# Batch-norm sums of a GNN kernel: products of a tile with itself on TensorE in place of column sums of values and squares

## What is computed

```python
h = a * x + node_out              # (N, D)
mu = h.mean(0)
var = h.var(0)
x = x + (h - mu) / jnp.sqrt(var + EPS) * g + be
```

## Time and profile before

| | |
|---|---|
| time, median of 3 runs | 6509.96 us (6462.72 to 6547.05) |
| span of the profiled execution | 5432.4 us |
| busy in it: PE, DVE, ACT, POOL | 4063.8 (75%), 3799.0 (70%), 2766.8 (51%), 3340.6 (61%) |
| statistics of layer 0, first to last DVE pass | 839.0 to 1003.5 us |
| statistics of layer 1, first to last DVE pass | 1787.3 to 1952.5 us |
| mean granted TensorE clock | 0.877 of full speed |

### The profile page before, as it was taken

The page is one execution under the profiler, slowest core; times in us unless marked ns, Lnnn a source line. Parts: engine busy times, 40 slices in busy tenths (PEclk is TensorE's granted clock), DMA queues, the critical chain, the costliest instruction groups (busy, mean ns, idle before and its releaser), DMA issues. The chain is left out here.

```text
span 5432.4 us, 61024 instructions
## 1 busy us (share of the span) xinstructions
PE 4063.8 (75%) x14777; PEld 2245.4 (41%) x14777; DVE 3799.0 (70%) x7522; ACT 2766.8 (51%) x5374; POOL 3340.6 (61%) x3399
## 2 busy tenths in 40 slices
PE   7854548402444866556989999999999989995697
PEld 4522223101222334444556555655565544553343
DVE  8986663698666368885878767876787677762276
ACT  7952222212222246656978547844784477544433
POOL 6757777776777737774357735700670066777677
PEclk9977669756776988888999999999999999997899
DMA  6743237884111789885878546754775377874455
GB/s 215 270 161 100 94 110 255 294 283 152 47 46 46 260 270 266 260 239 188 271 231 257 189 140 222 251 181 134 231 253 175 134 246 238 277 223 137 140 179 163
DMA packets 628091, 1062.84 MB, mean 196 GB/s; under 512 B 105048, under 2 KB 258158, under 8 KB 627740
## 3 DMA queue, kind: packets, MB, share of 16 engines
q1 hardware_dynamic: 498972, 818.46, 46.2%
q0 software_dynamic: 100544, 163.41, 10.8%
q10 hardware_dynamic: 28224, 77.08, 3.6%
HBM read 599.34 MB, written 464.81 MB: 196 GB/s over the span
## 5 line engine op out<-in xcount | busy, mean ns | idle before, releaser
L1891 POOL DMA_INDIRECT G<-msg_tab,srow x784 | 739.9, 944 | 914.2 <-issue 813.2
L878 PE MATMUL l_ps<-cv_V,cv_cwi 128*128 128x448 f32 x896 | 475.4, 698 | 769.4 <-DVEq L865 769.4
L878 PEld LDWEIGHTS l_ps<-cv_V,cv_cwi 128*128 128x128 f32 x896 | 218.9, 252 | 1026.4 <-issue 538.5
L1285 POOL DMA_INDIRECT x_tab<-a_r,node_pos x392 | 379.6, 968 | 200.6 <-issue 115.9
L2152 DVE TENSOR_TENSOR agg<-r_psS,agg 128x128 f32 x980 | 280.9, 287 | 285.2 <-PE r_psS L1998 211.8
L747 POOL DMA_INDIRECT o_tab<-cv_ob,put_idx x392 | 387.8, 989 | 122.8 <-issue 118.5
L1972 PE MATMUL r_psR<-r_hin,whh 128*128 128x512 f32 x882 | 454.1, 597 | 0.9 <-ACT r_ohn L2071 0.9
L739 POOL DMA_INDIRECT cv_M<-h_tab,gat_src x392 | 373.8, 953 | 119.4 <-issue 119.4
L1923 PEld LDWEIGHTS r_psM<-wmsg,r_hnew 128*128 128x128 f32 x2744 | 361.1, 192 | 169.6 <-issue 140.4
L1998 PE MATMUL r_psS<-r_sel,G 128*128 128x128 f32 x1960 | 297.7, 300 | 132.0 <-DMA G<-msg_tab,srow 131.2
L1923 PE MATMUL r_psM<-wmsg,r_hnew 128*128 128x128 f32 x2744 | 363.3, 276 | 3.9 <-DVE r_hnew L2216 3.9
(11 more groups left out here) (298 smaller groups left out, 10730.3 us busy)
## 6 DMA issues: line engine op xcount, KB each, us to landing
r_hin<-ht_tab SPq DMA_DIRECT2D x441, 256.0 KB
msg_tab<-r_m SPq DMA_DIRECT2D x392, 256.0 KB, 3.3
ht_tab<-r_hnew SPq DMA_DIRECT2D x343, 256.0 KB
o_tab<-o_blank SPq DMA_DIRECT2D x98, 512.0 KB, 5.0
st_h<-h_tab SPq DMA_DIRECT2D x98, 512.0 KB, 3.7
st_o<-o_tab SPq DMA_DIRECT2D x98, 512.0 KB, 4.7
r_oin<-ht_tab SPq DMA_DIRECT2D x161, 256.0 KB
i_x<-x_tab SPq DMA_DIRECT2D x49, 528.0 KB
```

The costliest lines, as they stand in the source:

```text
L878: ins = nc.tensor.matmul(psO[:, h, 0:HW], cwi[m][:], V[i % 2][m][:, HW * h:HW * (h + 1)], start=m == 0, stop=m == 3)
L1285: pool.indirect_dma_start(x2_tab, bass.IndirectOffsetOnAxis(ap=node_pos[:, j:j + 1], axis=0), rb[i % RR][:, t, :], None).then_inc(s_out[i ...
L1891: pool.indirect_dma_start(G[g % GR][:, q, :], None, msg_tab[s % 3], bass.IndirectOffsetOnAxis(ap=srow[:, j:j + 1], axis=0)).then_inc(s_g[g ...
```

## The change

The squares on ScalarE are gone, and so is `ones_last`. VectorE writes `a * h + o` to one of two new buffers `st_u` instead of in place. A row of `st_u` has for each of the eight nodes 128 values and a 129th column that holds 1.0, set once before the loop. TensorE takes for each node slot t the 128 x 128 tile of `st_u` as weights and the 128 x 129 tile (with the ones) as moving operand, and adds all 8 x 49 products up in one PSUM bank. The diagonal of the result is the sum of squares, its column 128 the sum of values, with one feature on each partition. In the last chunk both operands are cut to 106 partitions. At the end VectorE spreads both onto diagonals (by `ident`), and one matmul with `ones` as weights brings them to every partition, as they were before.

SP now waits for VectorE (`s_u`) and not for TensorE (`s_pe`) before it loads into a buffer again; VectorE waits for TensorE before it overwrites `st_u`. `slots` stands ahead of chunk 21 of `apply0`, not 18.

```diff
-            sq = [sb(f"{n}q{i}", [P, RT * D], F32, c) for i in range(2)]
+            ub = [sb(f"{n}u{i}", [P, RT, D + 1], F32, c) for i in range(2)]
-            psU, psQ = banks[0][:, 0:512], banks[1][:, 0:512]
+            psG, psB = banks[0][:, 0:D + 1], banks[1][:, 0:2 * D]
...
                     if i >= SR:
-                        sp.wait_ge(s_pe, i - SR + 1)
+                        sp.wait_ge(s_u, i - SR + 1)
                         sp.dma_start(hb[i % SR][:], hv[i]).then_inc(s_in[i % SR], 16)
...
+                for q in range(2):
+                    nc.vector.memset(ub[q][:, :, D:D + 1], 1.0).then_inc(s_one, 1)
                 for i in range(NCH):
                     k = i % SR
                     dve.wait_ge(s_in[k], 32 * (i // SR + 1))
-                    nc.vector.scalar_tensor_tensor(ob[k][:], hb[k][:], ab[layer][:, 0:1], ob[k][:],
-                                                   ALU.mult, ALU.add).then_inc(s_u, 1)
+                    if i >= 2:
+                        dve.wait_ge(s_pe, i - 1)
+                    nc.vector.scalar_tensor_tensor(
+                        ub[i % 2][:, :, 0:D], hb[k][:].rearrange("p (t f) -> p t f", f=D), ab[layer][:, 0:1],
+                        ob[k][:].rearrange("p (t f) -> p t f", f=D), ALU.mult, ALU.add).then_inc(s_u, 1)
                 dve.wait_ge(s_pe, NCH)
-                for q, ps in enumerate((psU, psQ)):
-                    st.mark(nc.vector.tensor_reduce(tot[:, q, :], ps.rearrange("p (t f) -> p f t", f=D),
-                                                    AX.X, ALU.add))
-                st.wait()
-                st.mark(nc.vector.tensor_scalar(tot[:], tot[:], 1.0 / N, None, ALU.mult))
+                nc.vector.tensor_scalar(tot[:, 0, :], ident[:], psG[:, D:D + 1], None, ALU.mult).then_inc(s_dg, 1)
+                nc.vector.tensor_tensor(tot[:, 1, :], psG[:, 0:D], ident[:], ALU.mult).then_inc(s_dg, 1)
+                dve.wait_ge(s_tot, 1)
+                st.mark(nc.vector.tensor_scalar(tot[:].rearrange("p q f -> p (q f)"), psB, 1.0 / N, None, ALU.mult))
...
             def scalar(act):
-                for i in range(NCH):
-                    act.wait_ge(s_u, i + 1)
-                    if i >= 2:
-                        act.wait_ge(s_pe, i - 1)
-                    nc.scalar.activation(sq[i % 2][:], ob[i % SR][:], ACT.Square).then_inc(s_q, 1)
-                act.wait_ge(s_dv, 6)
+                act.wait_ge(s_dv, 4)
                 nc.scalar.activation(rt[:], var[:], ACT.Sqrt, bias=epsc[:, 0:1]).then_inc(s_rt, 1)
 
             def tensor(pe):
+                pe.wait_ge(s_one, 2)
                 for i in range(NCH):
-                    w = ones_last if i == NCH - 1 else ones
-                    for t, s, ps in ((ob[i % SR], s_u, psU), (sq[i % 2], s_q, psQ)):
-                        pe.wait_ge(s, i + 1)
-                        for q in range(2):
-                            ins = nc.tensor.matmul(ps, w[:], t[:, 512 * q:512 * (q + 1)],
-                                                   start=i == 0 and q == 0, stop=i == NCH - 1 and q == 1,
-                                                   skip_group_check=True)
+                    m = LASTP if i == NCH - 1 else P
+                    pe.wait_ge(s_u, i + 1)
+                    for t in range(RT):
+                        ins = nc.tensor.matmul(psG, ub[i % 2][0:m, t, 0:D], ub[i % 2][0:m, t, :],
+                                               start=i == 0 and t == 0, stop=i == NCH - 1 and t == RT - 1,
+                                               skip_group_check=True)
                     ins.then_inc(s_pe, 1)
+                pe.wait_ge(s_dg, 2)
+                nc.tensor.matmul(psB, ones[:], tot[:].rearrange("p q f -> p (q f)"), start=True, stop=True
+                                 ).then_inc(s_tot, 1)
...
                 for i in range(NCH):
-                    if i == 18:
+                    if i == 21:
                         slots()
```

More of the change, by code:

```diff
@@ L136, in build @@
         ones = sb("ones", [P, P])
-        ones_last = sb("ones_last", [P, P])
         later = sb("later", [P, P])
@@ L411, in _ @@
                 st.mark(nc.vector.tensor_scalar(row0[:], ones[:], iota_p[:, 0:1], 0.0, ALU.mult, ALU.is_equal))
-                st.mark(nc.vector.tensor_scalar(ones_last[:], ones[:], iota_p[:, 0:1], float(LASTP),
-                                                ALU.mult, ALU.is_lt))
                 dve.wait_ge(s_src, 16 * 4)
@@ L489, in counts @@
                                          stop=True, skip_group_check=True).then_inc(s_cnt, 1)
-                pe.wait_ge(s_dv, 14)
+                pe.wait_ge(s_dv, 13)
                 turned(0)
@@ L887, in statistics @@
             s_u = stage_sem(n + "u")
-            s_q = stage_sem(n + "q")
             s_pe = stage_sem(n + "pe")
@@ L891, in statistics @@
             s_rt = stage_sem(n + "rt")
+            s_one = stage_sem(n + "ones")
+            s_dg = stage_sem(n + "diagonals")
+            s_tot = stage_sem(n + "totals")
             s_col = [stage_sem(n + "columns0"), stage_sem(n + "columns1")]
```

## The result

| | before | changed |
|---|---|---|
| time, median of 4 runs | 6486.37 us (6462.72 to 6547.05) | 6598.84 us (6552.55 to 6613.17) |
| ratio, 95% interval | | 1.0247 (1.0124 to 1.0369) |
| span of the profiled execution | 5432.4 us | 6611.4 us |
| statistics of layer 0, start of the first to start of the last DVE pass | 163 us | 345 us |
| statistics of layer 1 | 164 us | 222 us |

The ratio and its interval, as recorded, compare runs in the fast state alone and need not be the quotient of the medians, which is 1.017 here. The interval lies above 1, so the changed kernel is slower, but whether by more than 2% it leaves open.

What follows compares the result with a forecast made beforehand. TensorE was taken to set the statistics loops' pace, with POOL's chain limiting layer 0. Layer 1's -35 and layer 0's -11 gave -46 us: span 5386, median 6510 to 6464 us, range 6410 to 6530.

Steps and rivals of the forecast that it cites:

- the 1077.6 us around the span I leave as they are: Whole program: time outside the profiled span stays 1077.6 us, so the median of 6510 becomes 6464.
- what I don't see, such as the time around the span: Whole program: chance of 0.03 kept for unseen causes.
- sums and hand-over: End of layer 1's statistics and start of `apply1`: sums net +0.6 us, hand-over of loads +2 us (0 to 4).
- TensorE a chunk: Statistics loops: 3.43 us of matmuls removed, 16 instructions added, 1.79 us at full clock, 3.45 at half.
- DMA sets the pace: Statistics loops: loads become the limit, 2.8 us a chunk (375 GB/s), bounds 2.65 and 3.18.
- Rival 3: Statistics loops: weight loads of the 8 tiles not hidden, 4.8 us a chunk, time 6640; chance 0.03.
- rival 2: Statistics loops: TensorE's clock falls, 3.45 us a chunk at half clock, time 6500; chance 0.10.
- Rival 1: Statistics loops: DMA nearly full already, 3.18 us a chunk, 16 us less from layer 1, time 6480; chance 0.14.
- Layer 0 is cut off by POOL's chain: Layer 0: loop ends some 36 us earlier, but POOL's gathers and scatters limit the gain to -11 us (-7.5 to -13).
- Rival 4: Layer 0: gathers slowed more, 6480, or less, with VectorE's queue ending the block, 6450; chance 0.10, both signs alike.
- The shift of `slots`: `apply0`: moving from chunk 18 to 21 leaves three chunks less, 15 us, behind POOL's answer, allowing layer 0's gain.
- Wrong: no wait at `slots`: Layer 0: sign against the prediction, which expected VectorE to wait some 28 us for `look` ahead of `slots`.

Runs made afterwards that it cites:

- the mixture: Statistics of the kernel before in layer 0, changed ones in layer 1 with loads held by TensorE's count, `slots` at 21; 5406 to 5412 us, ratio 0.995, without late counts.
- experiment 2: The changed kernel with `slots` back ahead of chunk 18 of `apply0`; 6535.08 us, ratio 1.0178 (1.0099 to 1.0256).
- `b0`: The kernel before, unchanged, profiled again; median 6441.35 us, span 6441.5 us.
- experiment 5: The changed kernel, GpSimd waiting for the end of layer 0's statistics, all 196 gathers after, `slots` at 48; 6439.22 us beside 6473.87 for the kernel before, one run each.
- the paced GpSimd: The changed kernel with 42 gathers in layer 0's statistics, one a chunk, `slots` at 40; 5449 to 5452 us, ratio 1.002 to 1.003, without late counts.

## Why the prediction was wrong, point by point

**The step that failed** is "the 1077.6 us around the span I leave as they are". In every run that has both, span and time lie 2 to 3 us apart, so there is nothing around the span. The trace of the kernel before came from a job without late counts and its three times from one with them, so the sum was made on a program of 5432 us and the answer measured on one of 6486. What came in place of the step: in the measured kind of job the term that was to be layer 0's gain, a loop some 36 us shorter, was a loop 182 us longer, since the counts behind the 32 short instructions of a chunk came late and then passed at 1.40 us an instruction. The hint was in plain sight: a span 17% under the time, which the prediction put down to "what I don't see, such as the time around the span"; 0.03 for it was far too little. With such a gap the honest forecast is the sum for the kind of execution that the trace shows, and a wide, two-sided range for the other.

**The sum itself** can be judged where it applies, in the changed kernel's trace without late counts (`a_again`):
```profile
span 5377.9 us, 62507 instructions
```
The forecast was 5386 against 5432.4. VectorE there at the start and end of layer 1's statistics, and at the start of `apply1`:
```profile
1767.82 2.56 DVE L928 SCALAR_TENSOR_TENSOR st_u<-st_h,ab,st_o 128x1024 f32<-128x1024 f32 x2 [28.13 <-DMA st_o<-o_tab]
...
1890.86 1.28 DVE L928 SCALAR_TENSOR_TENSOR st_u<-st_h,ab,st_o 128x1024 f32<-128x1024 f32 x1 [1.25 <-DMA st_o<-o_tab]
...
1894.29 0.29 DVE L933 TENSOR_SCALAR st_tot<-ident,l_ps 128x128 f32<-128x128 f32 x1 [2.15 <-PE l_ps L964]
...
1894.84 0.70 PE L969 MATMUL l_ps<-st_tot,ones 128*128 128x256 f32 x2 [0.59 <-DVE st_tot L934]
...
1902.95 1.29 DVE L2275 SCALAR_TENSOR_TENSOR l_ps<-a_h,ab,l_ps 128x1024 f32<-128x1024 f32 x1 [3.00 <-ACT l_ps L1188]
```
Layer 0: the wait at `slots`, the first and last scatter of the block, and the next block's loads:
```profile
1097.70 0.26 DVE L1044 CAST pf<-look 128x196 f32<-128x196 int32 x1 [18.20 <-DMA look<-node_tab,src_at]
...
1102.70 1.02 POOL L673 DMA_INDIRECT sort_tab<-pair,sort_at  x1 [6.42 <-DVEq L1057]
...
1245.61 0.98 POOL L673 DMA_INDIRECT sort_tab<-pair,sort_at  x1 [0.30 <-issue]
1258.21 1.74 SPq L904 DMA_DIRECT2D st_h<-h_tab  x4
```
And two stretches, the loop of layer 1 and that of layer 0:
```profile
1790.00:1890.00 100.00, 78.45 (x612) 71.08 (x612) 49.48 (x39) 0.00 (x0) 64.18 (x65) 1.00 1.03 405
...
834.00:966.00 132.00, 98.22 (x763) 90.22 (x764) 61.65 (x48) 0.00 (x0) 102.53 (x97) 0.96 1.02 380
```

| term | forecast | measured |
|---|---|---|
| TensorE, 16 matmuls of a chunk | 1.79 us | 16 weight loads start and end within 1.86 us |
| chunk, set by DMA | 2.8 us (375 GB/s) | layer 1: 2.58 us, 405 GB/s; layer 0: 2.71 us, 380 GB/s |
| layer 1: the loop | 131, -33 | 1890.86 - 1767.82 = 123.0, -40.9 |
| last pass to sums | 3.2, -5 | 3.43, -4.75 |
| sums and hand-over (5.46 before) | +2.6 | 1902.95 - 1894.29 = 8.66, +3.2 |
| layer 1 in all | -35 | 135.13 against 177.59, -42.5 |
| VectorE stands at `slots` | 28 us | 18.2 us |
| next block starts | 1266 to 1268, -11 | 1258.21 against 1277.63, -19.4 |

-42.5 - 19.4 is -61.9; the span fell by 54.5, the other 7.4 lie behind the start of `apply1`, where one execution differs from the next by as much (the changed kernel's four runs span 12 us). By medians it is -64.4.

- **TensorE a chunk**: right, in form and size. Rival 3 (weights not hidden) falls; rival 2 falls too, the clock granted is 1.00 in the loop of layer 1.
- **DMA sets the pace**: right, and mis-sized. The value was put between two rows by choice; for layer 1 the four-microsecond burst of the earlier trace rows was the good guide (395 GB/s), the share 0.93 at 307 GB/s of the earlier trace rows, taken as a measure of what is left, was not: a share of 1.03 went with 405 GB/s. Rival 1 falls. The Trainium skill (DMA: Bandwidth & Descriptors, "Where 436 GB/s comes from") lets memory bind at about 358 GB/s for a core; this trace has 405 GB/s over 100 us, with GpSimd's scatters beside the loads, closer to the 425 it gives for a large single-core transfer, and the measurement decides.
- **Layer 0 is cut off by POOL's chain**: right as to the chain (wait at `slots`, scatters at once, 144 us of them, the next block behind them), but two of its terms were wrong and offset each other. Behind the last scatter the prediction had 2.1 to 4.9 us for its landing and nothing else. The trace has 11.6 us from its end to the next block (1246.59 to 1258.21), and most of that is a DRAIN on GpSimd. Before (line 1296) and changed (line 1297), with ScalarE's, which stands behind the last store:
```profile
L1296 POOLq DRAIN  x1: 9213/9213/9213, 1266.8 to 1266.8; - x1
L1296 ACTq DRAIN  x1: 8/8/8, 1276.7 to 1276.7; - x1
...
L1297 POOLq DRAIN  x1: 9213/9213/9213, 1248.0 to 1248.0; - x1
L1297 ACTq DRAIN  x1: 8/8/8, 1244.7 to 1244.7; - x1
```
Before, GpSimd was thus through at 1276.0 us and ScalarE at 1276.7: POOL's chain already ended the block as much as the last store did. With the scatters ending where the prediction left them (1262.6), 11.6 us more put the block's start at about 1274, an estimate, and the gain at 3 us instead of 11. The other term made up for it: mis-sized was what the statistics cost the gathers: 97 in 132 us, 1.36 us each, where 1.53 was carried over from the earlier trace rows. So `look` was complete 17 us earlier than before (1097.7 against 1114.7). Rival 4 had this as a case, though with VectorE's queue ending the block; it was GpSimd, through at 1257.2 us where ScalarE was at 1244.7. That the forecast of 11 and the measured 19 have the same sign is in part luck. The number of VectorE's passes was the same, so the premise that they alone make the gathers slow fails; in the mixture, with the old statistics, the last gather is issued at 1107.6 us, in the changed kernel at 1095.3.
- **The shift of `slots`** was to keep 15 us out of POOL's answer. In the measured kind of job it cost 13 us (experiment 2). Without late counts `slots` at 18 was not run; three more chunks (15 us) behind the last store at 1241.84 would have started the next block at about 1261 instead of 1258.21, an estimate, so the shift was worth 2 to 3 us there.
- **"Wrong: no wait at `slots`"** did show in the measured job, but for a reason that was not on the list: the loop took some 180 us more.

**Where the measured loss comes from.** Between the changed kernel (span 6611.4) and the re-profiled one before (6441.5) the stages differ by: the first convolution +5, layer 0's statistics +182, the apply stage behind them -22 and its surroundings +7 (in which the later `slots` has its 13), the second convolution +7, layer 1's statistics -6, `apply1` +10, the rest -11, near the difference of 170. It is layer 0: six steps there take 237 us, while the other 42 take 109 us, where all 48 took 163 before. These are two single executions, of different jobs; the medians of one job differ by 112 us, and the unchanged kernel alone spread from 6343 to 6670 us in a job with late counts.

**What stays open.** Why a job has late counts: of the jobs here, those whose results name their chip had them on chips 2 and 15, and were free of them on chips 1, 8 and 15, so chip 15 showed both. Why the backlog begins at pass 12 in one kernel, 16 or 19 in another, and in some loops not at all. Whether the paced GpSimd prevents it. And whether late counts exist in an execution that nobody records: each run of the experiments came with a span within 2 to 3 us of its time, so every time of theirs is of a recorded execution. The traces give this question weight. In that of the kernel before without late counts, 7322 of the 7326 semaphore updates of VectorE's instructions stand on record at the end of their instruction; in `b0`, with late counts, only 5318 of 7326. Those of the first 200 us, with no indirect transfer of GpSimd yet, are all there (757 of 757), and so are those of the loop of experiment 5 with GpSimd idle (48 of 48). So records of updates are missing in the kind of job and beside the transfers where TensorE's counts are late. That recording and late counts share a cause would fit this; no run here shows it.

## What to carry to other kernels

When the profile's span and the measured time differ by more than a few us, the profile may be of another kind of execution than the measurement, as it was here, and a sum made on it forecasts that other kind; take a second profile of the unchanged kernel before explaining a change. A loop that trades a few long TensorE instructions for many short ones can gain in one kind of execution and lose in the other, if GpSimd issues indirect transfers beside it: judge it on both. For a bandwidth that a loop will reach, a short burst with full queues was here a better guide than the share and rate of a loop that was held by something else. And follow each engine to the barrier of a block: what stands behind its last counted instruction, here 9.2 us on GpSimd, can decide when the next block starts.

## What the runs showed of the hardware that was not expected

- TensorE's semaphore counts can arrive up to 83 us after their multiplication while GpSimd issues indirect transfers back to back (one per 1.25 to 1.29 us), and then pass at 1.40 us for each TensorE instruction, weights and matmuls alike, until about 20 us after the last transfer (1155.0 to 1174.6 us in the changed kernel). Two loops with GpSimd idle had none of it in such jobs (122 us each).
- In all jobs here it was a property of the job: the kernel before takes 5436 or 6440 us, and one chip number has shown both.
- In a job without it, cutting TensorE's instructions in two (744 matmul records instead of 375 in 839 to 1003 us, layer 0's statistics) cost nothing that could be seen: 5437.15 against 5437.17 us.
- GpSimd's gathers took 1.36 us each beside the new statistics and 1.53 beside the old ones, with as many VectorE passes in both.
- The DRAIN that GpSimd has at the end of layer 0's block took 9.21 us in six traces, of both kinds of job, and in the changed kernel the next block waited for it.
